# A graph network layer pair on one core: the last visits of the second layer merged with its block work

## What is computed

```python
msgs = entity_emb[src_idx]                                   # x1, the output of layer 0
agg = segment_sum(msgs, dst_idx, num_segments=6250)
counts = segment_sum(ones, dst_idx, num_segments=6250)
agg = where(counts > 0, agg / maximum(counts, 1), agg)
tri_out = relu(agg @ W.T + b)
out = layernorm(x1 + tri_out)
```

## Time and profile before

| | us |
|---|---|
| median of 3 runs | 4301.83 |
| lowest and highest | 4300.47, 4306.43 |
| the profiled execution | 4298.34 |
| its span | 4296.2 |
| last gathered quad added (end of the last add) | 4144.92 |
| last visit added | 4185.19 |
| last statistics | 4260.83 |
| first store issued | 4269.17 |

### The profile page before, as it was taken

How to read it: one execution, slowest core, us unless ns; L and a number is a source line. 1 busy time by engine, 2 the same in 40 slices (tenths; PEclk the granted TensorE clock), 3 DMA queues, 4 the chain that set the end, 5 groups by cost and what they waited for, 6 DMA issues and landing times.

```text
span 4296.2 us, 78474 instructions
## 1 busy us (share of the span) xinstructions
PE 3223.5 (75%) x16047; PEld 2355.4 (55%) x16048; DVE 2682.6 (62%) x11914; ACT 1494.8 (35%) x2712; POOL 3005.4 (70%) x2631
## 2 busy tenths in 40 slices
PE   7657777777777777777777777879577777777775
PEld 3246666566656665666665666658444444444444
DVE  6356666666666666666666666858754555554555
ACT  2225545555545555554555555643100000000004
POOL 0258888888888888888888888751277777777734
PEclk9879989999999999998989899999788888888898
DMA  4665555555555555555555555585433333333324
GB/s 147 193 194 93 95 93 94 94 94 94 93 95 92 95 93 95 92 95 93 94 93 95 94 93 94 77 159 157 132 105 104 104 104 104 105 104 104 105 58 119
DMA packets 336078, 455.16 MB, mean 106 GB/s; under 512 B 53568, under 2 KB 282524, under 8 KB 335772
## 3 DMA queue, kind: packets, MB, share of 16 engines
q0 software_dynamic: 199680, 327.32, 41.6%
q1 hardware_dynamic: 116844, 105.48, 8.6%
q10 hardware_dynamic: 19248, 19.66, 1.3%
HBM read 296.41 MB, written 155.62 MB: 105 GB/s over the span
## 4 chain that ended last, share of the span: by engine, by line
POOL 35%; PE 21%; issue 20%; DMA 15%; DVE 5%; SPq 1%; ACT 1%; DVEq 1%; ACTq 0%; POOLq 0%
POOL sum L560 19%; POOL arena L549 14%; PE ps L846 9%; DMA arena<-x_tab,esrc 9%; DMA sum<-arena,sidx 3%; PE ps L849 3%; PE ps L800 2%; POOL arena L590 2%; PE ps L749 2%; DMA arena<-x_tab 1%; PE ps L712 1%; DMA arena<-loc_tab 1%; PE ps L818 1%; PE ps L736 1%; DVE arena L1526 1%
## 5 line engine op out<-in xcount | busy, mean ns | idle before, releaser
L560 POOL DMA_INDIRECT sum<-arena,sidx x832 | 1317.5, 1584 | 293.5 <-issue 248.7
L549 POOL DMA_INDIRECT arena<-p_tab,esrc x832 | 811.6, 975 | 448.4 <-issue 420.7
L590 POOL DMA_INDIRECT arena<-x_tab,esrc x832 | 794.4, 955 | 304.4 <-issue 146.0
L846 PE MATMUL ps<-arena 128*125 x1760 | 664.4, 465 | 340.2 <-DMA arena<-x_tab,esrc 298.3
L749 PE MATMUL ps<-w,arena 128*128 128x256 f32 x3328 | 838.5, 385 | 3.9 <-ACT arena L967 3.9
L846 PEld LDWEIGHTS ps<-arena 128*125 128x125 f32 x1760 | 380.1, 226 | 607.1 <-issue 521.0
L1325 DVE TENSOR_TENSOR arena<-ps,arena 128x256 f32 x880 | 373.5, 424 | 538.5 <-DMA arena<-p_tab,esrc 308.0
L1526 DVE TENSOR_TENSOR arena<-ps,arena 125x257 f32 x880 | 374.6, 426 | 507.0 <-PE ps L846 473.8
L749 PEld LDWEIGHTS ps<-w,arena 128*128 128x128 f32 x3328 | 571.8, 192 | 122.0 <-issue 5.2
L722 PE MATMUL ps<-ident,arena 128*128 128x128 f32 x1664 | 276.5, 320 | 461.1 <-DVE arena L1357 461.0
L712 PE MATMUL ps<-arena 128*128 128x256 f32 x1664 | 519.9, 469 | 2.7 <-ACT arena L957 2.5
(11 more groups left out here) (186 smaller groups left out, 3977.5 us busy)
## 6 DMA issues: line engine op xcount, KB each, us to landing
arena<-loc_tab SPq DMA_DIRECT2D x220, 125.0 KB
arena<-sum SPq DMA_DIRECT2D x200, 128.0 KB, 2.1
sum<-scr ACTq DMA_DIRECT2D x3, 6400.0 KB, 57.7
arena<-p_tab,esrc POOLq DMA_INDIRECT x832, 3.0
sum<-arena,sidx POOLq DMA_INDIRECT x832
arena<-x_tab,esrc POOLq DMA_INDIRECT x832, 2.8
sum<-scr SPq DMA_DIRECT2D x1, 6400.0 KB, 23.5
arena<-x_tab SPq DMA_DIRECT2D x50, 128.0 KB, 2.0
```

The lines of the kernel that those rows point to most:

```text
L549: pool.indirect_dma_start(out=ring0[:, tile % RING, :], out_offset=None, in_=p_tab[:, :], in_offset=bass.IndirectOffsetOnAxis(ap=esrc[:, t ...
L560: pool.indirect_dma_start(out=sums[u][:, :], in_=tot[:, par, u, :], in_offset=None, out_offset=bass.IndirectOffsetOnAxis(ap=sidx[:, par, u ...
L590: pool.indirect_dma_start(out=ring[:, tile % LATER_RING, 0:D], out_offset=None, in_=x1_tab[:, :], in_offset=bass.IndirectOffsetOnAxis(ap=e ...
L846: nc.tensor.matmul(ps[0:NB, u, 0:CW], same1[:, par, u, :], ring[:, bass.ds(at[u], 1), :].rearrange("p a c -> p (a c)"), start=True, stop=T ...
```

## The change

The last 12 quads of visits and the block work are put into one loop on all engines.

- PE: in quad 208 + j, after each visit u, it does block 4j - 2 + u (transpose of that block, projection of the one before). Four blocks stay behind the last visit. The filler matmul is left out in these quads. The transposes move to the banks `PP`, the projection to `PK`, since visits use banks 0 to 3.
- DVE: after each add it does result and statistics of block 4j - 6 + u, one quad behind PE. The counts are turned into reciprocals for 2 to 4 blocks at a time. After each tenth block it works out the scales of these ten (`group_scales`). It normalises only blocks 45 to 49.
- ACT: it normalises blocks 0 to 44, each 18 blocks behind its copy out of PSUM. POOL normalises none.
- SP: the loads of x1 no longer wait for the last visit. The stores of groups 0 and 1 stand behind loads 29 and 39, those of groups 2, 3 and 4 behind load 49.

```diff
-        NORM_ORDER = (("dve", GROUP, 0), ("act", GROUP, 2), ("dve", 2 * GROUP, 1), ("pool", GROUP, 4), ("act", 2 * GROUP, 3))
+        TAIL_QUADS = QUADS - TILE_QUADS
+        TAIL = TAIL_QUADS + 1
+        SHARE = BLOCKS - GROUP // 2
+
+        def whole_blocks(j):
+
+            return range(max(0, QT * j - 2), min(BLOCKS, QT * j + 2))
...
-            sp.wait_ge(e[1]["acc"], QUADS * QT)
-            steps(sp, BLOCKS, 0, load_1)
-            for done, count, g in NORM_ORDER:
-                sp.wait_ge(s_norm1[done], count)
-                store(g, out, s_out)
+            for q in range(BLOCKS):
+                load_1(q, q % 2)
+                if q % GROUP == GROUP - 1 and q >= 3 * GROUP - 1:
+                    g = q // GROUP - 2
+                    sp.wait_ge(s_norm1["act"], GROUP * (g + 1))
+                    store(g, out, s_out)
+            sp.wait_ge(s_norm1["act"], BLOCKS - GROUP)
+            store(BLOCKS // GROUP - 2, out, s_out)
+            sp.wait_ge(s_norm1["act"], SHARE)
+            sp.wait_ge(s_norm1["dve"], BLOCKS - SHARE)
+            store(BLOCKS // GROUP - 1, out, s_out)
...
-            pool.wait_ge(s_shift, 1)
-            for q in range(4 * GROUP, 5 * GROUP):
-                nc.gpsimd.tensor_scalar(rows[0:NB, q, 0:D], rows[0:NB, q, 0:D], momb[:, 1, q:q + 1],
-                                        nwb[:, 3, q:q + 1], ALU.subtract, ALU.mult).then_inc(s_norm1["pool"], 1)
...
-                    nc.tensor.matmul(ps[:, PK, :], identh[:, :], identh[:, :].unsqueeze(1).to_broadcast([P, QT, P]),
-                                     start=True, stop=True)
+                    if not isinstance(q, int) or q < TILE_QUADS:
+                        nc.tensor.matmul(ps[:, PK, :], identh[:, :],
+                                         identh[:, :].unsqueeze(1).to_broadcast([P, QT, P]), start=True, stop=True)
+                    beside(u)
...
-            for q in range(TILE_QUADS, QUADS):
-                aggregate(q, q % WIDE)
-
...
-            pe.wait_ge(e[1]["acc"], QUADS * QT)
-            for q in range(BLOCKS + 1):
-                block_1(q, q % 2)
+            for j in range(TAIL):
+                pe.wait_ge(e[1]["acc"], QT * (TILE_QUADS + j))
+                own = list(whole_blocks(j))
+
+                def beside(u):
+                    if u < len(own):
+                        block_1(own[u], own[u] % 2)
+                if j < TAIL_QUADS:
+                    aggregate(TILE_QUADS + j, (TILE_QUADS + j) % WIDE, beside)
+                else:
+                    for u in range(QT):
+                        beside(u)
+            block_1(BLOCKS, BLOCKS % 2)
...
+            def normalise_rows(q):
+                if q % GROUP == 0:
+                    ac.wait_ge(s_shift, q // GROUP + 1)
+                nc.scalar.activation(rows[0:NB, q, 0:D], rows[0:NB, q, 0:D], ACT.Identity,
+                                     bias=shiftb[:, q:q + 1], scale=nwb[:, 3, q:q + 1]).then_inc(s_norm1["act"], 1)
+            BEHIND_ROWS = GROUP + 8
+            for q in range(BLOCKS + BEHIND_ROWS):
                 if live(q, BLOCKS):
...
+                    columns_1(q, q % 2)
                 if live(q - 1, BLOCKS):
...
+                    mean(q - 1, (q - 1) % 2)
+                if live(q - BEHIND_ROWS, SHARE):
+                    normalise_rows(q - BEHIND_ROWS)
...
+            def counts(j):
+                own = whole_blocks(j)
+                a, z = own[0], own[-1] + 1
+                dve.wait_ge(s["acc"], QT * (TILE_QUADS + j))
+                nc.vector.tensor_scalar(cnt[:, 0, a:z], rows[0:NB, a:z, D], 1.0, None, ALU.max).then_inc(t["cnt"], 1)
+                dve.wait_ge(t["cnt"], 2 * j + 1)
+                nc.vector.reciprocal(cnt[:, 1, a:z], cnt[:, 0, a:z]).then_inc(t["cnt"], 1)
+
+            def group_scales(g):
+                own = slice(g * GROUP, (g + 1) * GROUP)
+                m, n = 7 * g, g * NEWTON_OPS
+                dve.wait_ge(t["stat"], (g + 1) * GROUP)
...
+            def whole_row(q):
+                result(q, q % 2, 1)
+                if q % GROUP == GROUP - 1:
+                    group_scales(q // GROUP)
+            for j in range(TAIL + 1):
+                if j < TAIL:
+                    counts(j)
+                before = list(whole_blocks(j - 1)) if j > 0 else []
+                if j < TAIL_QUADS:
+                    if j + 1 < TAIL_QUADS:
+                        one_hot_1(TILE_QUADS + j + 1, (j + 1) % 2)
+                    accumulate(TILE_QUADS + j, j % 2, lambda u: whole_row(before[u]) if u < len(before) else None)
+                else:
+                    for q in before:
+                        whole_row(q)
+            for q in range(SHARE, BLOCKS):
                 normalise(q, s_norm1["dve"])
```

More of the change, by code:

```diff
@@ L866, in columns_1 @@
                 for c in range(H):
-                    last = nc.tensor.transpose(ps[:, PZ + par, c * P:c * P + NB],
+                    last = nc.tensor.transpose(ps[:, PP + par, c * P:c * P + NB],
                                                rows[0:NB, q, c * P:(c + 1) * P], ident[0:NB, 0:NB])
@@ L875, in project @@
                 for c in range(H):
-                    last = nc.tensor.matmul(ps[0:NB, PM + par, 0:D], col[:, par, c, 0:NB], wt[:, c, :],
+                    last = nc.tensor.matmul(ps[0:NB, PK + par, 0:D], col[:, par, c, 0:NB], wt[:, c, :],
                                             start=c == 0, stop=c == H - 1)
@@ L1035, in _, with columns_1 @@
[L1035 to L1041, removed]
-                                         bias=shiftb[:, q:q + 1], scale=nwb[:, 3, q:q + 1]).then_inc(s_norm1["act"], 1)
+            def columns_1(q, par):
+                ac.wait_ge(t["cols"], q + 1)
+                if later(q, 2):
+                    ac.wait_ge(t["omm"], q - 1)
+                nc.scalar.activation(col[:, par, 0:H, 0:NB],
+                                     ps[:, PP + par, 0:H * P].rearrange("p (h n) -> p h n", h=H)[:, :, 0:NB],
+                                     ACT.Copy).then_inc(t["colev"], 1)
@@ new lines, in mean @@
+            def mean(q, par):
+                ac.wait_ge(t["cnt"], 2 * ((q + 2) // QT + 1))
+                ac.wait_ge(t["omm"], q + 1)
+                if later(q, 2):
+                    ac.wait_ge(s_biased, q - 1)
+                nc.scalar.activation(hpre[0:NB, par, :], ps[0:NB, PK + par, 0:D], ACT.Identity,
+                                     scale=cnt[:, 1, q:q + 1]).then_inc(s_mean, 1)
+            def normalise_rows(q):
[3 more added lines that the diff above has]
+                                     bias=shiftb[:, q:q + 1], scale=nwb[:, 3, q:q + 1]).then_inc(s_norm1["act"], 1)
@@ L1532, in step_1 @@
                     clear_rows()
-                if live(q, QUADS):
+                if live(q, TILE_QUADS):
                     accumulate(q, par)
-            steps(dve, QUADS, 0, step_1, ahead=1, by=4)
+            steps(dve, TILE_QUADS, 0, step_1, ahead=1, by=4)
             t = k[1]
-            dve.wait_ge(s["acc"], QUADS * QT)
-            nc.vector.tensor_scalar(cnt[:, 0, :], rows[0:NB, :, D], 1.0, None, ALU.max).then_inc(t["cnt"], 1)
-            dve.wait_ge(t["cnt"], 1)
-            nc.vector.reciprocal(cnt[:, 1, :], cnt[:, 0, :]).then_inc(t["cnt"], 1)
@@ L1543, in _ @@
-            dve.wait_ge(t["cnt"], 2)
-            def block_1(q, par):
-                result(q, par, 1)
-            steps(dve, BLOCKS, 0, block_1, by=4)
-            block_scales()
-            dve.sem_inc(s_shift, 1)
-            nc.vector.scalar_tensor_tensor(out=shiftb[:, :], in0=momb[:, 1, :], scalar=-1.0, in1=nwb[:, 3, :],
-                                           op0=ALU.mult, op1=ALU.mult).then_inc(s_shift, 1)
-            for q in range(2 * GROUP):
+            def counts(j):
[5 more added lines that the diff above has]
+                nc.vector.reciprocal(cnt[:, 1, a:z], cnt[:, 0, a:z]).then_inc(t["cnt"], 1)
```

42 lines of the change are left out of this document (25 added, 17 removed).

## The result

| | median us | lowest to highest |
|---|---|---|
| before | 4301.20 | 4300.47 to 4306.43 |
| changed | 4270.11 | 4265.70 to 4271.00 |

The ratio is 0.9927 with an interval of 0.9914 to 0.9939: faster by 0.7%, where 0.6% was forecast. The forecast was 4275, the range 4266 to 4290.

A forecast was written before the change was run, and what follows sets the result against it. Four stretches in a row, without overlap, bound the tail. Merged loop to 4241.9, last rows, scales and stores gave span 4266.7; plus clock 2.1 and loads 0.5, 4269.3; 26.9 us below profiled, so 4275 from the median, range 4266 to 4290.

The forecast's parts named there:

- rivals 2, 3 and 4: Merged loop: loads end last, 4284 (0.07); slots add up, 4296 (0.08); TensorE stays at 1.2 GHz, 4324 (0.05).
- signs of being wrong: Merged loop: DVE waits for PE's visits each slot, clock near 0.5, or x1 loads release results inside quads.
- Quads of 7.35 us: Merged loop, quads 2 to 10: DVE takes 0.5 + 0.85 + 6.0 us each, nine times, 66.2 us.
- Scales, 14.4 us: Merged loop, after rows 9, 19, 29, 39: four ten-column chains of 3.6 us each on DVE, uncovered.
- The clock, 2.1 us: Merged loop, four places where scales stand: PE idles about 4.4 us, slow start delays second visit 0.6 us each.
- rival 1: Merged loop: clock drops in most quads, not four; up to 10 us more, time 4283, chance 0.15.
- Fillers worth nothing: Last visits: dropping 48 filler matmuls alone gains nothing, since PE waits for DVE after them anyway.
- Stores beside loads, 0.5 us: SP's queue: stores of groups 0 and 1 delay loads by 0.5 us together, ends 0 and 10.
- Rows 42 to 49: Behind the last visit: eight rows bound by loads, 2.75 us a pair; row 49 ends at 4252.7.
- The end: Behind the last statistics: last scales 3.6 us, normalising 2.5, last three stores; 14.0 us where 35.4 stood before.
- Both roads: At the end: three stores in a row finish at 4264.7, the last store issued after scales at 4264.1.
- The sum's split of the gain: Whole change: 8.1 us from joining the loops, 21.4 from the end, 2.6 given back to clock and loads.

The follow-up runs named there:

- the kernel that holds the clock: Changed kernel plus filler matmuls only in the four places where PE idles longest, and two waits reordered: 4266.72 us, ratio 0.9918.
- spread scales: Changed kernel with scale-chain steps of groups 0 to 3 issued singly over the next five slots, and an unused DVE signal dropped: 4266.58 us, ratio 0.9910.
- the second half of the change: Run alone against the kernel before: two loops and fillers kept, but scales by ten, rows normalised on ACT, stores between loads: 4290.70 us, ratio 0.9975.
- the kernel with four loads: Changed kernel with four buffers for loads of x1 instead of two, and the signal between result and statistics dropped: 4265.63 us, ratio 0.9909.

## Why the prediction held, point by point

The time and the direction came as forecast, and so did the overlap of the two loops and the short end; rivals 2, 3 and 4 did not. But two terms of the sum were wrong and cancelled, so that the closeness of the number is luck. One of the prediction's own signs of being wrong came too: inside a quad DVE waits for PE's visits.

- *Quads of 7.35 us.* Mis-sized. They take 6.6 us. The step that failed is the slot of 0.46 + 0.58 + 0.46 = 1.50 us on DVE: an add may follow statistics after 0.34 us and a result may follow an add after 0.34, so that a slot is 1.26. With it DVE needs 0.5 + 0.85 + 5.0 = 6.4 us and PE 6.6, as its own sum said. "DVE sets the pace with 0.8 us to spare" was wrong: PE does, by 0.2 us a quad. The adds did stand 1.5 us apart, as forecast, but for another reason. The twelve quads without chains take 78.0 us (79.8 in a second profile), where 82.6 stood in the sum.
- *Scales, 14.4 us.* Right as the operations go: four chains of 3.4 us, 13.6, and 14.2 by the kernel that holds the clock.
- *The clock, 2.1 us.* The mechanism was right, in its places (behind the chains, and nowhere else; the fourth falls behind the last add) and as a matter of half clock. The size was not: 6.8 us in one execution and about 3 in the other. The step that failed is that a slow start costs DVE only where the second visit is late by 0.6 us. That held for a PE with 0.8 us to spare in each quad; with none to spare, most of what PE loses moves the loop (17.1 us at half clock are 8.5 us of matmuls lost, and the loop is 6.8 longer). It was also wrong to see PE's wait only at the end of a quad. It waits in the middle too, through ACT, POOL and DVE. In one execution it is 4.7 us more than the term, within the "up to 10 us more" of rival 1, though only in the quads behind a chain, and in the other about 1.
- Together: 82.6 + 14.4 + 2.1 = 99.1 us was said, 98.9 measured, as 78.0 + 14.2 + 6.8 within rounding. The terms missed by 4.6 too much and 4.5 too little.
- *Fillers worth nothing.* Right, shown by the kernel before without them.
- *Stores beside loads, 0.5 us.* Right here: 0.3 and 0.9 us of waiting at row 29 in the two profiles, none without the stores, and nothing in the medians. It holds for this pace only, as the spread scales show. They left at 4212.8 and 4233.9, where 4210 and 4231 were said.
- *Rows 42 to 49.* 11.6 us from the last add to the last statistics, 10.8 said. DVE waits 1.3 us for loads there. With four buffers and without the signal it is 10.2, so the loads are only a part of it.
- *The end.* 14.4 us, 14.0 said. Both roads, three stores in a row and the last store behind the last scales, end close together, as said.
- *The sum's split of the gain* (8.1 us from merging, 21.4 from the end) came out for this kernel: 5.4 us from the loops, where 8.1 less 2.6 stood, and 20.9 from the end. As a reason it misleads: merging alone gives 24 to 27 us, and the second half of the change is paid for by what it adds to the loop, 17 to 21 us. By itself it gave 9.7 us, since in the block loop, where DVE was idle for 31 us of 76, its chains added 11 us, and beside the merged loop it gave nothing that can be measured.

## What to carry to other kernels

A step that is moved into a loop to shorten the end can cost its full length there when two engines are within a few per cent of each other, as here 6.4 and 6.6 us a quad; then test it in the merged loop, and not only against the old one. Price a sequence of operations by the nearest rows with the same neighbours: start to start of two vector operations was 0.34 to 0.46 us by what stood ahead, and three such steps made the wrong engine look like the bound. Where two loops are merged, a long chain on one engine sends an idle time round the ring of all others, and here PE's clock made it dearer by 3 to 7 us. And when a loop gets faster, look again at what was hidden in it: a store beside the loads was free in the changed kernel and cost up to 2.7 us in the faster one.

## What the runs showed of the hardware

In the kernel with spread scales a vector operation on 10 columns took 0.16 us behind an add or a result, and 0.54, as a median, right behind the statistics of a 256-wide row. A mean over all of them hides it. One semaphore signal between result and statistics went with 0.13 us between their starts (0.58 with it, 0.45 without), in kernels that differ in other things too.

PE held its higher clock at 71% of busy time without fillers in one stretch of 40 us (its longest wait was 1.5 us), and lost it at 82% in another of 99 us, with waits of 1.9 to 3.8 us. A wait of 1.87 us before a projection, in the kernel with four loads, was not followed by slow matmuls, and one of 1.88 in the changed kernel was. The kernel before without the last fillers even had a wait of 3.38 us, at the end of its gather stage, without a fall:

```profile
4143.64 0.69 PE L846 MATMUL ps<-arena 128*125 x2 [3.38 <-DMA arena<-x_tab,esrc]
4144.17 0.38 PE L850 MATMUL ps<-identh 128*128 128x512 bf16 x1
4144.39 0.60 PE L846 MATMUL ps<-arena 128*125 x2
```

The kernel before had one of 3.42 us at the same place, and slow visits behind it. So the length of the wait alone does not decide.
